# Second attention layer: query projection, and second part of the key projection, ahead of a row tile's scores

## The reference

```python
q = _split_heads(jnp.einsum('bnd,df->bnf', x, Wq))
kv = jnp.einsum('bmc,cf->bmf', context, Wkv)
k, v = jnp.split(kv, 2, axis=-1)
k = jnp.concatenate((nk, k), axis=-2); v = jnp.concatenate((nv, v), axis=-2)
sim = jnp.einsum('bhid,bhjd->bhij', q * scale, k)
out = jnp.einsum('bhij,bhjd->bhid', jax.nn.softmax(sim, axis=-1), v)
out = jnp.einsum('bnf,fd->bnd', out, Wout)      # then a layer norm and a gated residual
x = x + jnp.tanh(g_ffn[1]) * _L1_ffn_ref(...)   # eight experts, two for each token
```

## Time and profile before

| | us |
|---|---|
| median of 3 runs (1825.55 to 1828.7) | 1825.76 |
| the profiled execution | 1830.33 |
| its span, first to last instruction | 1828.6 |
| PE busy in the span | 1696.2 (93%) |
| DVE busy | 1195.2 (65%) |
| ACT busy | 1045.7 (57%) |

### The profile page before, as it was taken

The page is one execution under the profiler, slowest core; times in us unless marked ns, Lnnn a source line. Parts: engine busy times, 40 slices in busy tenths (PEclk is TensorE's granted clock), DMA queues, the critical chain, the costliest instruction groups (busy, mean ns, idle before and its releaser), DMA issues.

```text
span 1828.6 us, 27461 instructions
## 1 busy us (share of the span) xinstructions
PE 1696.2 (93%) x9294; PEld 1082.1 (59%) x9294; DVE 1195.2 (65%) x2830; ACT 1045.7 (57%) x2160; POOL 375.5 (21%) x374
## 2 busy tenths in 40 slices
PE   5899998899799899999999999999998888999998
PEld 3455555455455345444554455444645788999997
DVE  3867876876778667555567457664676688666632
ACT  2467666666666656655555546555455466666621
POOL 2101110120011010000000000200021467777721
PEclk9899999999999999999999999999999899999999
DMA  3000000010003009200000000100001757777775
GB/s 104 1 24 1 1 24 1 1 28 3 1 1 138 2 2 347 73 24 1 1 1 23 1 1 1 58 2 1 13 25 56 227 148 218 214 210 198 218 230 161
DMA packets 121147, 127.10 MB, mean 70 GB/s; under 512 B 9904, under 2 KB 116400, under 8 KB 121008
## 3 DMA queue, kind: packets, MB, share of 16 engines
q1 hardware_dynamic: 113280, 116.68, 20.2%
q0 software_dynamic: 7152, 8.66, 2.6%
q10 hardware_dynamic: 576, 0.00, 0.0%
HBM read 96.46 MB, written 29.77 MB: 69 GB/s over the span
## 4 chain that ended last, share of the span: by engine, by line
PE 53%; DVE 5%; DVEq 1%; issue 1%; SPq 1%; ACT 0%; DMA 0%; POOLq 0%
PE psum L2497 8%; PE psum L1845 6%; PE psum L1716 6%; PE psum L1700 6%; PE psum L1722 5%; PE psum L1831 5%; PE psum L2515 4%; PE psum L1707 3%; PE psum L2472 3%; PE psum L1756 2%; PE psum L2482 1%; DVE moe_w_lo L2615 1%; DVE l_k_lo L2109 1%; DVE l_k_hi L2107 1%; PE psum L2454 0%
## 5 line engine op out<-in xcount | busy, mean ns | idle before, releaser
L1273 DVE TENSOR_REDUCE l_tile_max<-psum 128x1 f32<-128x512 f32 x512 | 342.1, 689 | 109.9 <-PE psum L951 108.2
L1121 ACT ACTIVATE l_probs<-psum 128x1024 f32<-128x1024 f32 x256 | 248.3, 1022 | 105.7 <-PE psum L963 102.0
L951 PE MATMUL psum<-l_kT,l_qT 128*128 128x512 f32 x512 | 238.3, 473 | 40.1 <-DVE l_tile_max L1273 36.8
L2049 DVE TENSOR_REDUCE l_row_max<-psum 128x2 f32<-128x1024 f32 x124 | 151.6, 1223 | 140.7 <-PE psum L1700 139.9
L2784 POOL TENSOR_TENSOR moe_w_lo<-moe_w,moe_w_hi 128x512 fp32r<-128x512 f32 x128 | 179.9, 1407 | 92.7 <-ACT moe_w_hi L2568 91.6
L951 PEld LDWEIGHTS psum<-l_kT,l_qT 128*128 128x128 f32 x512 | 98.0, 192 | 132.3 <-DVE l_tile_max L1273 111.7
L1888 ACT ACTIVATE l_probs<-psum,l_neg_max 128x512 f32<-128x512 f32 x248 | 167.2, 674 | 0.0
L963 PE MATMUL psum<-l_qT,l_kT 128*128 128x512 f32 x512 | 160.4, 397 | 1.7 <-ACT l_probs L1121 1.5
L1831 PEld LDWEIGHTS psum<-ident,l_probs 128*128 128x128 f32 x1024 | 120.5, 143 | 68.8 <-issue 53.1
L2599 ACT ACTIVATE moe_gate<-psum 128x256 f32<-128x256 f32 (+1 forms) x184 | 64.7, 352 | 158.7 <-PE psum L2497 98.5
L2497 PE MATMUL psum<-moe_xs_hi,moe_w_hi 128*128 128x256 f32 x512 | 148.0, 289 | 1.4 <-DVE moe_xs_lo L2625 1.4
(11 more groups left out here) (361 smaller groups left out, 3278.6 us busy)
## 6 DMA issues: line engine op xcount, KB each, us to landing
moe_w<-in_moe_w SPq DMA_DIRECT2D x276, 256.0 KB, 4.6
moe_sorted_x<-l_null_cols SPq DMA_DIRECT2D x1, 17680.0 KB, 56.4
moe_xs<-moe_sorted_x SPq DMA_DIRECT2D x16, 272.0 KB, 2.9
moe_w<-in_ctx SPq DMA_DIRECT2D x8, 512.0 KB, 3.6
moe_w<-in_ctxT SPq DMA_DIRECT2D x4, 1024.0 KB, 5.7
moe_w<-in_wkv SPq DMA_DIRECT2D x2, 2048.0 KB, 15.7
x_resid<-in_x SPq DMA_DIRECT2D x4, 512.0 KB, 11.0
out_x<-x_resid SPq DMA_DIRECT2D x4, 512.0 KB, 4.4
```

Source lines behind the costliest of these rows:

```text
L951: nc.tensor.matmul(bank(max_bank(m)), qT[:, q % SLOTS, h, t * P:(t + 1) * P], kT[:, q % SLOTS, h // 2, half * BANK:(half + 1) * BANK], sta ...
L1121: nc.scalar.activation(probs[:, n % PT_RING], wide(2 * (n % 2)), ACT.Exp, scale=SCALE).then_inc(exp_done, 1)
L1273: nc.vector.reduce_max(tile_max[:, q % 2, t, h, half:half + 1], bank(max_bank(m)), AX_X).then_inc(max_read, 1)
L2049: nc.vector.reduce_max(row_max[:, t, :], wide(2 * (t % 2)).rearrange("p (j m) -> p j m", j=2), AX_X)
```

## The change

In round 0 TensorE issues the query projection ahead of the scores, in round 2 the second half of the key projection ahead of the scores; in rounds 1 and 3 nothing moves. VectorE reads these two fills ahead of the round's maxima. ScalarE's order stays. No instruction is added or removed.

```diff
                 for i in range(GROUPS):
                     for r in range(4):
+                        if r == 0:
+                            fill((i, r, 0))
+                        if r == 2 and i + 2 < GROUPS:
+                            project_keys(i + 2, range(s.CC // 2, s.CC)).then_inc(misc_psum, 1)
                         if i + 1 < GROUPS:
                             scores(i + 1, r)
-                        fill((i, r, 0))
-                        if r == 2 and i + 2 < GROUPS:
-                            project_keys(i + 2, range(s.CC // 2, s.CC)).then_inc(misc_psum, 1)
+                        if r != 0:
+                            fill((i, r, 0))
                         transpose_probs(i, r)
...
                 for i in range(GROUPS):
                     for r in range(4):
-                        if i + 1 < GROUPS:
-                            maxima(i + 1, r)
                         if r == 0:
                             read_fill((i, 0, 0))
                         if r == 2:
                             read_fill((i, 1, 0))
+                        if i + 1 < GROUPS:
+                            maxima(i + 1, r)
                         if i + 1 < GROUPS and r >= 1:
                             normalize(i + 1, r - 1)
```

## The result

The changed kernel is slower: 1854.52 us, median of 4 runs (1853.7 to 1857.69), against 1827.21 us for the kernel before (1825.55 to 1828.7, 4 runs). The ratio is 1.0153, 95% interval 1.0135 to 1.017. The two profiled executions have spans of 1856.0 and 1828.6 us, so 27.4 us more are to be found between the two traces.

A forecast was written before the change was run, and what follows sets the result against it. TensorE, busy 93% of the span, was taken as the bound, with the side chain perhaps next. Terms 5.2 + 3.8 + 2.3 + 3.7 + 3.7 + 2.9 - 4.6 = +17.0 us on 1825.76 gave 1842.8 us, range 1828 to 1858.

The forecast's parts named there:

- the eighteen waits: TensorE's waits before fills, fourteen for `l_k_lo` (0.7 us each), four for `l_q_lo` (0.6 us), all go: at most -11.8 us.
- small stall to round 1: Round 1's transposes wait 0.2 us for the later `keep_probs(i, 0)` in 26 groups: +5.2 us, bounds 0 and 18.
- groups 0 and 2: No fill hides the later `keep_probs(i, 2)`, so the group's last transposes wait: +1.7 and +2.1, together 3.8 us.
- groups 8, 16, 24: Last transposes start at x + 7.67 instead of x + 6.92, x being round 2's start: 3 x 0.75 = 2.3 us.
- groups 5, 13, 21 and 15, 23, 29: Fill (i, 3, 0), or the same pattern with `rT`, waits for ScalarE's read behind `keep_probs`: 3.7 us for each three groups.
- groups 16 and 24, round 0: Round 1's key projection waits for ScalarE's `rT` read behind `keep_probs(i, 0)`, 1.4 us later: 2.9 us together.
- null scores and `logits` (five waits): Waits in groups 6, 14, 22 (null scores) and 17, 25 (`logits`) count as saved: 5 x 0.68 us.
- `prefix` (19, 27): The waits before the `prefix` fills in groups 19 and 27 count as saved: 2 x 0.6 us.
- Both rivals: Half-clock stretches vanish with the waits: 6.8 us less, 1836 us (11%); or clock falls in ten places: 17 more, 1860 (14%).
- The transposes behind both come no earlier or later by themselves: On TensorE, scores (0.89 us) and projection (1.82 us) swap with the round's total for both unchanged at 2.71 us.
- Only the waits go: Rival: the side chain has more room than counted, so the waits are pure gain: 1814 us, chance 7%.
- it cancels: Rival: delays in 13 places stay, 26 small stalls don't come, half-clock stretches vanish: +5.0, 1829 us, chance 6%.

The follow-up runs named there:

- the early read: The changed kernel, but in round 0 VectorE reads the fill (i, 0, 1) ahead of its extra steps: 1852.76 us, ratio 1.0144.
- the one with round 2 alone: The kernel before with only the change's round 2 part, on both engines, round 0 as before: 1846.71 us, ratio 1.0117.
- The late fills: The kernel before with the fills at (i, 0, 1) and (i, 2, 1) behind `weigh_values`, on TensorE alone: 1819.21 us, ratio 0.9945.

## Why the forecast was right, and where it was not

Direction and mechanism held: the eighteen waits went, and delays through `keep_probs` outweighed them. The size did not: forecast +17 us, measured +27. 1854.52 us lies in the wide range, 1828 to 1858 us, but above the 1835 to 1850 us of the forecast's own case; the margin given to stalls and clock covered a term that was not in the sum. Step by step, with the change's own cost for a fourth shape taken out of each group's difference:

| term | forecast, us | measured, us |
|---|---|---|
| small stall to round 1, 26 rounds | +5.2 | 26 x 0.09 = +2.3 |
| groups 0 and 2 | +3.8 | 1.58 + 1.91 = +3.5 |
| groups 8, 16, 24 | +2.3 | 3 x (1.47 - 0.74 - 0.15) = +1.7 |
| groups 5, 13, 21 and 15, 23, 29 | +7.4 | 6 x (1.96 - 0.75 - 0.15) = +6.4 |
| groups 16 and 24, round 0 | +2.9 | 2 x (1.90 - 0.68 - 0.15) = +2.1 |
| null scores and `logits` (five waits) | -3.4 | 5 x (-0.83 - 0.15) = -4.9 |
| `prefix` (19, 27) | -1.2 | 2 x (1.22 - 0.73 - 0.15) = +0.7 |
| fourth shape change, 60 rounds | 0 | 60 x 0.15 = +9.0 |
| clock | 0 (rivals) | +3.5 |

These make 24.3 us. Of the other 3 us, 0.7 lie ahead of the layer (its first matmul is at 685.18 instead of 684.49) and 1.9 behind the last `weigh_values`; they were not taken apart.

- *Readiness of everything on VectorE and ScalarE* came out to 0.01 us, since all durations and their order were in rows. Each line of listed places is 1 us or less off. A wait shown as 0.7 us turned out worth 0.9 to 1.0 us a group when it went (0.76 and 0.83 measured, and the 0.15 us that hide a part).
- *"The transposes behind both come no earlier or later by themselves"* is the step that failed. I added the durations 0.89 and 1.82 us as if they did not depend on what follows. A sum over moved pieces has to be taken over the transitions, and a fourth shape change was there to be counted in the code. The round's total is 4.84 us, not the unchanged 4.69: with 60 such rounds it is the largest missed term, 9.0 us. "Busy time is the same on all engines" fell with it. The first half of the key projection put ahead of the scores alone shows the 0.15 us without a wait, and the second half put behind the transposes ties it to the fourth change.
- *`prefix`* was forecast with the wait for `l_q_lo` gone and nothing behind it. In group 19 the maxima, now late, push the output statistics, and these the prefix's read; the key projection then waits 1.4 us. Shown by the early read.
- *The small stall* was too large: I compared `keep_probs` with the old 7.40 us, while the round itself had become 0.15 us longer. And the weight load that "can slip by 0.4 us at no cost" cost 0.05 us: the transposes take 1.09 us without it ahead, 1.04 with it.
- *Clock.* Both rivals came true in part. The stretches at 1.2 GHz behind null scores went in groups 6, 14 and 22 (to round 3, -1.28 to -1.35 us), and others came behind waits of 1.9 us, in 13, 15, 21, 23 and 29. Added up over windows of 2 us up to the end of group 30, 8.5 us of full clock were lost before and 12.0 in the changed kernel's profiled execution. They fall elsewhere in each kernel: in the one with round 2 alone group 15 has +1.97, not +3.66 us. The rule that I had named (the Trainium skill, TensorE: Matmul & The Clock Gate, "A second HAM failure mode: psum-queue depth-cycling") points the right way here, at 3.5 us of 27.
- *Only the waits go* had the Trainium skill on its side (Perfetto Trace Analysis, Optimization Strategy: find what ends the gap and make it start sooner). The waits did go, but the time rose by 1.5%: here the earlier dependency was bought with a later one. The late fills leave the dependency where it was, move the waiting piece instead, and gain 0.55%.
- *Sums.* Two figures of the forecast do not follow from its own terms: "it cancels" is 1825.76 + 5.0 = 1830.8 us, not 1829, and the wide range comes to 1831 to 1856 us, not 1828 to 1858. The result lies inside either.

## What to carry to other kernels

When a piece is put ahead of another on a full engine, list who reads the one that is now late and follow it to its last reader in every in-order queue, above all where a copy that frees a PSUM bank stands behind it. Here a wait was cheaper to remove by letting the waiting piece step behind ready work than by making its input earlier; try both. Count changes of the tile's shape in TensorE's order before and after: adding up durations as they stood did not show them here.

## What was not expected of the hardware

A change between 64 x 128, 128 x 128 and 128 x 64 matmuls in f32 costs TensorE time that is booked as busy: one more of them a round made it 4.84 instead of 4.69 us. In round 0 of group 10 before, the first weight load of the transposes runs 0.43 us ahead of their matmuls, behind a piece of the same shape and without a wait; where the shape changes, it starts with the matmuls (scores at 910.66 and 910.67, transposes at 921.18, both above).
